# Sixteen batches through four conditioned blocks on one core: the second batch's weights kept in SBUF, and the last product of the third block as three products over rounded operands

## The chip, the cores and the metric

The program runs on one core of a Trainium2 chip. Time is the device time of one execution in microseconds (us); of several executions the median counts. The core's engines are called here as the profile calls them: PE is TensorE with its matmuls, PEld its weight loads, ACT is ScalarE, DVE is VectorE, POOL is GpSimd, and SP issues all DMAs of this kernel.

## What is computed

Sixteen batches (256 rows by 256 columns each) go through four blocks one after the other. A batch never meets another. Cut to what matters:

```python
# block A: weights of its own for each batch, made from cond (64 numbers a batch)
Wd_b = Wd + 0.1 * (cond @ Wdd.T + bdd)        # (16, 128, 256): 32768 numbers a batch
Wu_b = Wu + 0.1 * (cond @ Wdu.T + bdu)        # as many
x = x + relu(x @ Wd_b.T + bd) @ Wu_b.T + bu
x = (layernorm(x) * w + bias + tanh(cond @ lin_w.T + lin_b)) * w + bias
# third block: modulated attention with 16 heads of 16, then a feed-forward part
h = layernorm(x) * g1 + b1;  q, k, v = split(h @ W_qkv.T + b_qkv)
x = x + (softmax(q k' / 4) v @ W_o.T + b_o) * a1
h = layernorm(x) * g2 + b2
x = x + (gelu_tanh(h @ W_f1.T + b_f1) @ W_f2.T + b_f2) * a2      # 256 -> 1024 -> 256
# fourth block
u = (x * (scale * rsqrt(mean(x*x)))) @ up_w.T;  val, gate = split(u)   # 256 -> 2048
h = val * gelu(gate)
y = quantised(h) @ ternary(down_w).T + x
```

## The kernel before

**Operands.** Most products are wanted more exactly than one product of rounded operands gives. For these the operands are split: `hi` is the number rounded to the type F32R, `lo` what is left of it, and the function `three` (L500 to L505) adds three products, hi by hi, lo by hi and hi by lo. In the profile such a product shows as three matmuls "f32" of one instruction each at L504. A product of plain F32 operands is written as one matmul, and the profile counts two matmul instructions for each. The second feed-forward product of the third block (`c_g`, L713) is of that plain kind: 16 matmuls a batch, 32 instructions, 512 in all. The hi copy is made by ACT (`ACT.Copy` into an F32R tile), the lo part by POOL (`low_part`, a subtraction) for `hA`, `hC` and `hD`, the inputs of three products.

**Turns.** The work of a batch is cut in four stages: A (block A, the second block, and q, k, v), B (attention), C (output product, the feed-forward part) and D (fourth block). Turn t holds stage A of batch t, B of t-1, C of t-2 and D of t-3, so there are 19 turns, 0 to 18. In which order each engine does the slices of a turn is written by hand in the tables `HEAD` (turns 0 to 5), `FULL` (one table, for turns 6 to 12) and `TAIL` (12 to 18). A name such as `C.g0` is a slice: stage C, the quarter 0 of the last product. On PE the four slices `C.g0` to `C.g3` of `c_g` stand between slices of attention: `B.t` (scores, transposed), `B.o` (times v). `C.f0` to `C.f3` make the 1024 hidden columns, `C.ht` and `C.xt` are transposes, `D.u0` to `D.u3` the 2048 columns of block four, `D.qt` and `D.y` its last product, `A.down`, `A.up`, `A.ht`, `A.q`, `A.k`, `A.v` stage A. Engines wait for each other by semaphores that count the steps of a stage; the lists `ACT_C`, `POOL_C` and so on name the steps.

**ACT and DVE in a turn.** ACT takes the relu (`A.down`), the two norms (`lnb`), the modulations and hi copies (`ht`, `xt`), the tanh gelus (`C.f`, tile `G`), the exact gelus (`D.u`, tile `gl`), q and k (`A.q`, `A.k`), the exponentials (`B.t`) and the copies `D.qt`. DVE multiplies `gl` by the value half (`D.u`, step `h`, tile `hd`), quantises (`D.quant`), takes the maxima of the scores (`B.s`) and makes the lo parts of q and k. `D.qt0` on PE waits for step `h3` of DVE, which comes after `D.u3`. The gated output of `c_g` goes DVE (`gate2`) then POOL (`x3`).

**The head.** The weights of all batches are generated from `hyper` (16 chunks of 1 MB) into the tile `gen`, which lies where `wup_hi` will be. The first batch's share goes from `gen` to the tile `cur` in 16 small DMAs (`first_rows`). The whole of `gen` is then stored to DRAM in four DMAs of 1 MB (L402), and `cur` of every later batch is loaded from there (`load_weights`, L391) and combined with the shared part by DVE (`A.cur`, function `combine`, L1056). Then SP loads W_qkv, W_f1, W_up, W_f2 and W_down. Each of the first three has a hi copy on ACT (`W.qkv`, `W.fa`, `W.up`) and a lo part on DVE (L1040).

## Time and profile before

| what | us |
|---|---|
| median of 3 runs | 893.33 |
| lowest and highest of them | 892.43, 893.88 |
| the profiled execution | 892.32 |
| its span in the trace | 890.5 |
| PE busy in the span | 814.7 |
| PEld, DVE, ACT, POOL busy | 629.9, 551.0, 520.9, 235.1 |

The span is what the trace covers; 1.8 us of the profiled execution lie around it. PE's busy time is made of modelled ends, since matmuls are pipelined: how long a matmul really takes of PE is read from the distance of two starts, not from its duration. The granted clock of PE in forty slices is about 0.5 of full in the first tenth of the span, after its first two slices, and 1.0 from a fifth of it on.

### The profile page before, as it was taken

The page shows a single profiled execution, that of the slowest core. Times are in us where ns is not written, and L with a number is a line of the kernel's source. Part 1 is how long each engine was busy: PE and PEld are TensorE (multiplying, and loading weights), DVE is VectorE, ACT ScalarE, POOL GpSimd, SP SyncE. Part 2 cuts the span into 40 slices and gives each one's busy share as a digit, 9 for nine tenths or more (in the row PEclk, how much of TensorE's full clock was granted, in tenths as well). Part 3 has the DMA queues.
Part 4 walks back from the last instruction along what each step waited for, and adds up shares of the span by engine and source line. Part 5 has one row for each costly group of instructions (what it writes and reads, how often), then busy time and mean ns, then how long its engine had stood idle before and what let it go on. Part 6 is the DMA issues. An engine that isn't in the chain of part 4 may idle for free.

```text
span 890.5 us, 15833 instructions
## 1 busy us (share of the span) xinstructions
PE 814.7 (91%) x5852; PEld 629.9 (71%) x5852; DVE 551.0 (62%) x1063; ACT 520.9 (58%) x808; POOL 235.1 (26%) x333
## 2 busy tenths in 40 slices
PE   6862477999999999999999999999999999999976
PEld 4212346777787878787878787878788787877665
DVE  1322567686767768585858585858585767656424
ACT  1112243566676758585867667666667676765642
POOL 1002213050505142423223140505050505030310
PEclk9855577999999999999999999999999999999999
DMA  9989733334242342424251514234242333230100
GB/s 346 382 309 409 234 130 112 117 113 150 71 163 72 110 135 85 160 85 161 84 162 52 178 64 151 94 117 129 102 139 102 119 114 107 102 101 3 31 13 12
DMA packets 56093, 118.48 MB, mean 133 GB/s; under 512 B 6000, under 2 KB 11504, under 8 KB 53312
## 3 DMA queue, kind: packets, MB, share of 16 engines
q1 hardware_dynamic: 56016, 117.48, 38.7%
q8 instruction: 46, 0.75, 0.3%
q14 instruction: 31, 0.25, 0.1%
HBM read 82.51 MB, written 34.16 MB: 131 GB/s over the span
## 4 chain that ended last, share of the span: by engine, by line
PE 80%; issue 8%; DVE 4%; DMA 3%; POOL 3%; ACT 1%; SPq 1%; POOLq 0%; DVEq 0%; ACTq 0%
PE bank L504 31%; PE bank L713 13%; PE pair_s L668 6%; PE pair_t L504 5%; PE bank L679 3%; PE bank L760 3%; PE pair_s L656 3%; PE pair_s L634 3%; DMA hyp<-in_hyper 2%; PE bank L572 2%; PE bank L578 2%; PE pair_t L656 2%; PE bank L752 2%; PE pair_t L634 1%; PE pair_t L514 1%
## 5 line engine op out<-in xcount | busy, mean ns | idle before, releaser
L713 PE MATMUL bank<-wf,G 128*128 128x256 f32 x512 | 126.6, 391 | 0.7 <-ACT G L885 0.5
L504 PE MATMUL bank<-wup_hi,hD_hi 128*128 128x512 f32 x256 | 110.2, 430 | 4.1 <-POOL hD_lo L1333 3.2
L1361 POOL TENSOR_TENSOR x<-x,xcr 128x512 f32<-128x512 f32 x16 | 20.8, 1301 | 335.4 <-DVE x L1198 335.4
L870 ACT ACTIVATE Pr<-pair_s 128x1024 f32<-128x1024 f32 x64 | 65.6, 1025 | 74.8 <-PE pair_s L656 74.8
L713 PEld LDWEIGHTS bank<-wf,G 128*128 128x128 f32 x512 | 92.2, 189 | 21.8 <-issue 5.8
L504 PE MATMUL bank<-wup_hi,hD_lo 128*128 128x512 f32 x256 | 101.6, 397 | 0.0
L504 PE MATMUL bank<-wup_lo,hD_hi 128*128 128x512 f32 x256 | 101.5, 396 | 0.0
L1140 DVE TENSOR_REDUCE nmax<-pair_s 128x4 f32<-128x1024 f32 x64 | 77.9, 1218 | 20.4 <-PE pair_s L634 20.3
L1164 DVE STREAM_TRANSPOSE oq<-pair_s 128x512 f32<-128x512 f32 x32 | 22.9, 717 | 88.7 <-PE pair_s L668 88.7
L1140 DVE TENSOR_REDUCE nmax<-pair_t 128x4 f32<-128x1024 f32 x64 | 77.4, 1210 | 0.0
L914 ACT ACTIVATE gl<-bank,rsD 128x512 f32<-128x512 f32 x64 | 43.8, 684 | 52.7 <-PE bank L504 52.5
L1208 DVE SCALAR_TENSOR_TENSOR hd<-bank,rsD,gl 128x512 f32<-128x512 f32 x64 | 47.8, 747 | 32.0 <-PE bank L504 30.8
L668 PE MATMUL pair_s<-Pr,Va 128*32 128x256 f32 x1024 | 65.1, 396 | 0.3 <-ACT Pr L870 0.2
L870 ACT ACTIVATE Pr<-pair_t 128x1024 f32<-128x1024 f32 x64 | 65.2, 1019 | 0.0
L504 PEld LDWEIGHTS bank<-wup_hi,hD_hi 128*128 128x128 f32 x256 | 48.3, 189 | 18.8 <-POOL hD_lo L1333 3.4
L504 PEld LDWEIGHTS bank<-wup_lo,hD_hi 128*128 128x128 f32 x256 | 48.4, 189 | 11.7
L504 PEld LDWEIGHTS bank<-wup_hi,hD_lo 128*128 128x128 f32 x256 | 48.6, 190 | 9.7
L668 PEld LDWEIGHTS pair_s<-Pr,Va 128*32 128x32 f32 x1024 | 29.6, 112 | 26.6 <-ACT Pr L870 8.4
L922 ACT ACTIVATE qT<-bank 128x1024 bf16<-128x1024 bf16 x32 | 32.8, 1024 | 23.6 <-PE bank L752 23.6
L504 PE MATMUL bank<-hA_hi,wqkv_hi 128*128 128x256 f32 x128 | 39.9, 312 | 3.4 <-POOL hA_lo L1333 3.4
L504 PE MATMUL bank<-hC_hi,wf_hi 128*128 128x256 f32 x128 | 38.1, 298 | 3.6 <-POOL hC_lo L1333 3.6
L1333 POOL TENSOR_TENSOR hA_lo<-hA,hA_hi 128x512 fp32r<-128x512 f32 x16 | 20.6, 1285 | 75.9 <-ACT hA_hi L849 75.9
(183 smaller groups left out, 2000.4 us busy)
## 6 DMA issues: line engine op xcount, KB each, us to landing
hyp<-in_hyper SPq DMA_DIRECT2D x16, 1024.0 KB, 8.6
Qp<-qk_scratch SPq DMA_DIRECT2D x64, 256.0 KB, 4.9
Kp<-qk_scratch SPq DMA_DIRECT2D x64, 256.0 KB, 4.7
qk_scratch<-q_hi SPq DMA_DIRECT2D x16, 512.0 KB, 2.8
qk_scratch<-k_hi SPq DMA_DIRECT2D x16, 512.0 KB, 3.4
tC<-rows_scratch SPq DMA_DIRECT2D x16, 384.0 KB, 4.3
xT_t<-in_xT SPq DMA_DIRECT2D x16, 256.0 KB, 4.3
x_t<-in_x SPq DMA_DIRECT2D x16, 256.0 KB, 4.5
```

Of the source, the lines that this page charges most:

```text
L504: mm = pe.matmul(dst, l, r, start=first and i == 0, stop=last and i == 2)
L634: mm = pe.matmul(pair[p % 2][:, half, r * L:(r + 1) * L], Qp[lo:lo + KR, 1 - par, p, r * P:(r + 1) * P], Kp[lo:lo + KR, 1 - par, p, :], st ...
L656: mm = pe.matmul(pair[p % 2][:, half, k * L:(k + 1) * L], Kp[lo:lo + KR, 1 - par, p, k * P:(k + 1) * P], Qp[lo:lo + KR, 1 - par, p, :], st ...
L668: mm = pe.matmul(bank[1][32 * j:32 * j + 32, (g % 2) * L:(g % 2 + 1) * L], Va[:, 1 - par, k, 4 * g + j, :], Pr[:, (2 * g + j // 2) % 4, j ...
L679: mm = pe.matmul(bank[5][:, r * D:(r + 1) * D], oT[:, k, r * P:(r + 1) * P], wo[:, k, :], start=k == 0, stop=k == KT - 1)
L713: mm = pe.matmul(bank[5][:, r * D:(r + 1) * D], G[:, k, r * P:(r + 1) * P], wf2[:, k, :], start=k == 0, stop=k == FT - 1)
L760: mm = pe.matmul(bank[6][:, 0:D], qT[:, k, :], wq3[:, k, :], start=k == 0, stop=k == FT - 1)
L870: act.activation(Pr[:, p % 4, :, :].rearrange("p a n -> p (a n)"), pair[p % 2][:, :, :].rearrange("p a n -> p (a n)"), ACT.Exp, scale=DH * ...
L914: act.activation(gl[:, n % 2, :], bank[6][:, :], ACT.Gelu, scale=rsD[:, 1, n // 2:n // 2 + 1]).then_inc(act_d, 1)
L922: act.activation(qT[:, :, :].rearrange("p k n -> p (k n)"), bank[7][:, :].bitcast(BF16), ACT.Copy).then_inc(act_d, 1)
L1140: dve.tensor_reduce(nmax[:, n % 2, :, p % GP, :], pair[p % 2][:, :, :].rearrange("p a (r n) -> p a r n", r=RT), AX.X, ALU.max, negate=True ...
L1208: dve.scalar_tensor_tensor(hd[:, (n % 2) * HALF:(n % 2 + 1) * HALF], bank[7][:, :], rsD[:, 1, n // 2:n // 2 + 1], gl[:, n % 2, :], ALU.mul ...
```

## The change

There are four kinds of edits.

1. **The last feed-forward product in three.** `c_g` calls `three` with `G_hi`, `G_lo`, `wf2_hi`, `wf2_lo`. ACT copies `G` to `G_hi` in two halves (`C.gh0`, `C.gh1`), POOL subtracts in four quarters (`C.gl0` to `C.gl3`). W_f2 is split once, in turn 1 and 2 (`W.f2` on ACT and POOL). `C.g0` waits for the second quarter, `C.g1` for the fourth.
2. **The second batch's weights.** `first_rows` also copies the rows of batch 1 to a tile `second`, and `combine(1)` reads that. The DMAs of the first and of the second batch's rows stand side by side. The load of W_qkv is ahead of the last four of them. The stores of `gen`, W_f1 and W_up are issued within turn 0, W_f2 and W_down at the start of turn 1.
3. **Memory.** `hA`, `hC`, `hD`, `G` and the raw W_f2 lie on their lo parts, `sq` on `G_hi`, `gated` on `hC_hi`; `xcr` and `ys` are gone, and `x3` is used in their place. The ones beside v in `Va` are one column a head and no longer sixteen. POOL's `C.proj` therefore waits for the stores of the batch before last.
4. **Order.** The tables are new. In most turns PE does `C.f3` ahead of `B.m0` and `A.ht`, `D.qt0` ahead of `A.q`, and `B.t0` ahead of `A.v`.

```diff
-                        mm = pe.matmul(bank[5][:, r * D:(r + 1) * D], G[:, k, r * P:(r + 1) * P], wf2[:, k, :], start=k == 0, stop=k == FT - 1)
+                        mm = three(bank[5][:, r * D:(r + 1) * D], (G_hi[:, k, r * P:(r + 1) * P], G_lo[:, k, r * P:(r + 1) * P]),
+                                   (wf2_hi[:, k, :], wf2_lo[:, k, :]), k == 0, k == FT - 1)
...
+                    if n == 0:
+                        pe.wait_ge(pool_c, at(POOL_C, "glo1", c))
+                    elif n == 1:
+                        pe.wait_ge(pool_c, at(POOL_C, "glo3", c))
...
+                def c_gh(h):
+                    act.wait_ge(act_c, at(ACT_C, f"gelu{4 * h + 3}", c))
+                    act.activation(G_hi[:, 4 * h:4 * h + 4, :], G[:, 4 * h:4 * h + 4, :], ACT.Copy).then_inc(act_c, 1)
...
+                def c_gl(i):
+                    pool.wait_ge(act_c, at(ACT_C, f"ghi{i // 2}", c))
+                    pool.tensor_tensor(G_lo[:, 2 * i:2 * i + 2, :], G[:, 2 * i:2 * i + 2, :], G_hi[:, 2 * i:2 * i + 2, :].bitcast(F32),
+                                       ALU.subtract).then_inc(pool_c, 1)
+
+                def f2_weights():
+                    pool.wait_ge(act_w, at(ACT_W, "f2", 0))
+                    pool.tensor_tensor(wf2_lo[:, :, :], wf2[:, :, :], wf2_hi[:, :, :].bitcast(F32), ALU.subtract).then_inc(pool_w, 1)
...
                 sp.dma_start(cur[8 * c:8 * c + 8, :], gen[0:P:NB, c, :]).then_inc(first_in, 16)
+                sp.dma_start(second[8 * c:8 * c + 8, :], gen[1:P:NB, c, :]).then_inc(second_in, 16)
...
-                    dve.wait_ge(cur_in, 16 * b)
+                    dve.wait_ge(cur_in, 16 * (b - 1))
                 dve.wait_ge(dve_w, at(DVE_W, "base", 0))
-                dve.scalar_tensor_tensor(cur[:, :], cur[:, :], DELTA, base_c[:, :], ALU.mult, ALU.add).then_inc(cur_ready, 1)
+                dve.scalar_tensor_tensor(cur[:, :], second[:, :] if b == 1 else cur[:, :], DELTA, base_c[:, :], ALU.mult, ALU.add).then_inc(cur_ready, 1)
...
-                    past(pool, pool_c, POOL_C, "x3", c, 1)
-                    pool.tensor_tensor(xcr[:, :, :], xc[:, :, :], over_rows(tC[:, 2, :]), ALU.add).then_inc(pool_c, 1)
+                    if c >= 2:
+                        for r in range(RT):
+                            pool.wait_ge(y_out[r], 16 * (c - 1))
+                    pool.tensor_tensor(x3[:, par, :, :], xc[:, :, :], over_rows(tC[:, 2, :]), ALU.add).then_inc(pool_c, 1)
```

**DVE in the head**, from the end of batch 0's second norm on. `cur<-cur` is `combine(1)`, `q_lo` and `k_lo` are the lo parts that PE's `A.v` and the stores wait for, `wup_lo` is the lo part of W_up. Before:

```order
L1099 BN_AGGR mvA<-stA 128x2 x2
L1040 TENSOR_TENSOR wqkv_lo<-wqkv_raw,wqkv_hi 128x1536
L1056 SCALAR_TENSOR_TENSOR cur<-cur,base_c 128x512
L1132 SCALAR_TENSOR_TENSOR q_lo<-bank,small,q_hi 128x256 x2
L1040 TENSOR_TENSOR wf_lo<-wf_raw,wf_hi 128x2048
L1132 SCALAR_TENSOR_TENSOR k_lo<-bank,small,k_hi 128x256 x2
```

And now, up to the first maximum of turn 1:

```order
L1139 BN_AGGR mvA<-stA 128x2 x2
L1096 SCALAR_TENSOR_TENSOR cur<-second,base_c 128x512
L1077 TENSOR_TENSOR wqkv_lo<-wqkv_raw,wqkv_hi 128x1536
L1172 SCALAR_TENSOR_TENSOR q_lo<-bank,small,q_hi 128x256 x2
L1172 SCALAR_TENSOR_TENSOR k_lo<-bank,small,k_hi 128x256 x2
L1077 TENSOR_TENSOR wf_lo<-wf_raw,wf_hi 128x2048
L1146 TENSOR_TENSOR x<-bank,x_t 128x512
...
L1139 BN_AGGR mvA<-stA 128x2 x2
L1077 TENSOR_TENSOR wup_lo<-wup_raw,wup_hi 128x4096
L1180 TENSOR_REDUCE nmax<-pair_s 128x2x2
```

The combination for batch 1 reads `second`, W_f1's part is behind `k_lo`, and W_up's part (behind `q_lo` of turn 1 before) is ahead of the first maximum of turn 1.

**ACT in the middle of an inner turn**, from the first tanh gelus on. `x<-x,rsA` is the norm `A.lnb`, `gl` the gelu of `D.u3`. Before:

```order
L885 ACTIVATE G<-bank,small 128x256 x2
L832 ACTIVATE x<-x,rsA 128x256 x2
L885 ACTIVATE G<-pair_t,small 128x256 x4
...
L849 ACTIVATE hA_hi<-hA 128x512
L914 ACT_TABLE_LOAD
L914 ACTIVATE gl<-bank,rsD 128x512
L885 ACT_TABLE_LOAD
L885 ACTIVATE G<-bank,small 128x256 x2
L856 ACTIVATE q_hi<-bank,small 128x256 x2
L922 ACTIVATE qT<-bank 128x1024
L856 ACTIVATE k_hi<-bank,small 128x256 x2
```

And now:

```order
L917 ACTIVATE G<-bank,small 128x256 x2
L917 ACTIVATE G<-pair_t,small 128x256 x2
L865 ACTIVATE x<-x,rsA 128x256 x2
L922 ACTIVATE G_hi<-G 128x1024
L917 ACTIVATE G<-pair_t,small 128x256 x2
L860 ACTIVATE hA<-bank,mod 128x256 x2
L881 ACTIVATE hA_hi<-hA 128x512
L949 ACT_TABLE_LOAD
L949 ACTIVATE gl<-bank,rsD 128x512
...
L957 ACTIVATE qT<-bank 128x1024
L888 ACTIVATE q_hi<-bank,small 128x256 x2
L922 ACTIVATE G_hi<-G 128x1024
```

A copy of 128x1024 stands ahead of the gelus of `C.f2`, of A's modulation and of the gelu of `D.u3`; the second one is between q and k, and `D.qt0`'s copy has come ahead of q.

## Rows read from the trace of the kernel before

**Rows 1.** Stretches: length, busy of PE, PEld, DVE, ACT, POOL; clock, DMA share.
```profile
0.00:100.00 100.00, 57.53 (x238) 26.71 (x238) 23.99 (x51) 16.10 (x27) 12.35 (x23) 0.71 0.92 349
...
484.00:535.00 51.00, 51.00 (x391) 41.20 (x390) 35.90 (x68) 35.54 (x56) 14.34 (x20) 1.00 0.31 107
```
**Rows 2.** Costliest groups: busy us, mean ns of one, idle before.
```profile
L713 PE MATMUL bank<-wf,G 128*128 128x256 f32 x512 | 126.6, 391 | 0.7 <-ACT G L885 0.5 <-DVE k_lo L1132 0.3
...
L504 PEld LDWEIGHTS pair_t<-hC_hi,wf_lo 128*128 128x128 f32 x128 | 24.6, 193 | 0.0
```
**Rows 3.** PE in order of time, two inner turns: start, duration, line, tiles.
```profile
508.11 1.03 PE L572 MATMUL bank<-xT_t,cur 128*128 128x256 f32 x4
...
522.12 0.28 PE L504 MATMUL bank<-hC_hi,wf_hi 128*128 128x256 f32 x1
...
526.26 0.28 PE L504 MATMUL pair_t<-hC_lo,wf_hi 128*128 128x256 f32 x1
...
528.23 0.28 PE L504 MATMUL bank<-hC_lo,wf_hi 128*128 128x256 f32 x1
528.43 0.50 PE L634 MATMUL pair_s<-Kp,Qp 64*128 64x256 f32 x4
```
**Rows 4.** PE in order of time, round the first slice of the product.
```profile
539.43 1.99 PE L713 MATMUL bank<-wf,G 128*128 128x256 f32 x8
541.35 0.50 PE L656 MATMUL pair_s<-Qp,Kp 64*128 64x256 f32 x4
...
554.81 1.03 PE L572 MATMUL bank<-xT_t,cur 128*128 128x256 f32 x4
```
**Rows 5.** ACT in order of time, same turn: table, exact gelu, exponential.
```profile
529.02 1.28 ACT L914 ACT_TABLE_LOAD   x1
530.79 0.69 ACT L914 ACTIVATE gl<-bank,rsD 128x512 f32<-128x512 f32 x1 [0.50 <-PE bank L504]
...
539.31 1.03 ACT L870 ACTIVATE Pr<-pair_s 128x1024 f32<-128x1024 f32 x1 [0.80 <-PE pair_s L656]
```
**Rows 6.** DVE in order of time: step h3, and two twin steps of turn 2.
```profile
532.19 0.75 DVE L1208 SCALAR_TENSOR_TENSOR hd<-bank,rsD,gl 128x512 f32<-128x512 f32 x1 [0.85 <-PE bank L504]
...
146.79 0.87 DVE L1114 SCALAR_TENSOR_TENSOR x<-x,mvA,w_t 128x256 f32<-128x256 f32 x2
147.79 1.89 DVE L1121 SCALAR_TENSOR_TENSOR x<-x,rsA,tA 128x256 f32<-128x256 f32 x2
```
**Rows 7.** PE in turn 3, where `D.qt0` follows `B.s3` already.
```profile
205.11 0.40 PE L634 MATMUL pair_t<-Kp,Qp 64*128 64x256 f32 x4
205.69 0.62 PE L752 MATMUL bank<-identb,qi 128*128 128x128 bf16 x8 [0.18 <-DVE hd L1208]
```
**Rows 8.** POOL in order of time: inner turn, turn 2, and turn 0.
```profile
551.65 1.28 POOL L1361 TENSOR_TENSOR x<-x,xcr 128x512 f32<-128x512 f32 x1 [21.29 <-DVE x L1198]
...
148.12 1.28 POOL L1333 TENSOR_TENSOR hC_lo<-hC,hC_hi 128x512 fp32r<-128x512 f32 x1 [1.31 <-ACT hC_hi L879]
...
70.41 1.71 POOL L1301 TENSOR_TENSOR rsA<-mvA,eps_ln 128x2 f32<-128x2 f32 x1
```
**Rows 9.** PE in the head, turns 0 to 2.
```profile
93.76 0.58 PE L504 MATMUL bank<-wqkv_hi,hA_hi 128*128 128x256 f32 x1 [10.21 <-DVE q_lo L1132]
...
102.08 0.80 PE L634 MATMUL pair_s<-Kp,Qp 64*128 64x256 f32 x4
...
137.94 1.90 PE L679 MATMUL bank<-wo,oT 128*128 128x256 f32 x8
```
**Rows 10.** DVE in the head: the combination for batch 1, and W_up's lo part.
```profile
92.23 0.69 DVE L1056 SCALAR_TENSOR_TENSOR cur<-cur,base_c 128x512 f32<-128x512 f32 x1 [20.16 <-DMA cur<-cur_scratch]
...
121.72 4.40 DVE L1040 TENSOR_TENSOR wup_lo<-wup_raw,wup_hi 128x4096 fp32r<-128x4096 f32 x1
```
**Rows 11.** SP's issues: the load of batch 1's `cur`, and the store of `k_lo`.
```profile
77.56 0.34 SPq L391 DMA_DIRECT2D cur<-cur_scratch  x1
...
96.72 0.32 SPq L420 DMA_DIRECT2D qk_scratch<-k_lo  x1
```

235 lines of the change are left out of this document (131 added, 104 removed).

## Prediction, made before the run

> **What bounds the kernel now.** Read first the busy time of the engines by stretch [rows 1]: in the inner turns PE is busy in all 51.00 us of a 51 us stretch at full clock, DVE and ACT in 70% of it, POOL in 28%. That busy share is made of modelled ends, so the second thing to read is the distance of starts. A turn, from `A.down` to `A.down`, is 554.81 − 508.11 = 46.70 us [rows 3, 4], and in those rows one PE slice starts where the one before it ends. So in turns 3 to 15 what is taken from PE is taken from the time, unless a wait comes in its place. The head is another matter: in the first 100 us PE has work for 57.53 us at a mean clock of 0.71 while the DMAs are 92% busy [rows 1], and it stands still 10.21 us for `q_lo` [rows 9]. That wait is read through: `q_lo` is behind `combine(1)` on DVE, which itself waited 20.16 us for the load of `cur` [rows 10], and that load was issued at 77.56 [rows 11], behind 4 MB of stores, W_f1, W_up, W_f2 and W_down in SP's program.
>
> **The product in three (PE).** Before, a slice of four products holds PE from 539.43 to 541.35, 1.92 us or 0.24 for each of its 8 instructions [rows 4]; all 512 make 123 us. After, it is 12 matmuls of the shape that `C.f` has already, 128x256 with a new weight each. The 36 of `C.f0` to `C.f2` start 0.118 us apart (522.12 to 526.26 in 35 steps), but it is 0.20 where the attention's matmul follows (528.23 to 528.43), so the switch costs about 0.08 [rows 3]. A slice is 12 × 0.118 + 0.08 = 1.50 us: 0.42 less, and 1.7 us for the four slices of a turn. More instructions (768 for 512), less time.
>
> **What feeds it.** ACT gets two copies of 128x1024 a turn. None is in the trace; the exponential of that size takes 1.03 and a gelu of half the size 0.69 [rows 5]; I take 1.0 each. POOL gets four subtractions of 128x512 at 1.28 [rows 8], 5.1 us a turn; it was idle 21.29 us just ahead of `x3` [rows 8], where most of them go. `C.g1` waits for the fourth: from PE's end of `A.q` the chain is q's two copies 0.85, `gh1` 1.0, two subtractions 2.6 and some 0.4 of latencies, 4.9 us, while PE does `A.k`, `B.m1`, `D.y0`, `B.t0`, `A.v`, `C.g0` and `B.t1`, 6.7 us. Nothing waits. If `gh1` were 2 us later, `C.g1` would wait 0.2.
>
> **The new order in the turn.** The first copy, `gh0`, is ahead of the gelus of `C.f2`, of A's modulation and of `D.u3`'s gelu on ACT. Before, the table for that gelu began at 529.02 and the gelu waited for PE only 0.50 [rows 5]. With `C.f3` ahead of `A.ht` PE comes to `D.u3` at the same time as before, about 528.9, and is done with its first half at 530.3, but ACT, 1.0 us fuller and with the norm behind `C.f1`, loads the table at about 530.3 and gives the gelu from 531.6 to 532.3. `h3` on DVE takes 0.75 [rows 6] and ends at about 533.1. PE has done `D.u3` and `B.s3` by 532.4 and now wants `D.qt0` at once; before it had `A.q` there. So about 0.7 us of PE are lost. Turn 3 of before has this order: there 205.11 to 205.69 are 0.58 us where 0.33 are usual, a loss of 0.25, without the copy [rows 7]. Against that, `C.f2` with `C.f3` and `A.q` with `A.k` now stand together, which saves some switches: 0.3 us for four, and the remaining gaps of this stretch, 0.2. A turn gains 1.7 + 0.5 − 0.7 = 1.5 us. Bounds: 0.8, if the norm's delay of 1.2 (it stands behind `B.s3` on DVE) adds to the stall; 2.1, if the stall is the 0.25 of turn 3 or less. Other edits of the turn are at nothing: the aliasing puts waits on steps that ended a turn ago; POOL comes to its wait for the stores after `x2` of the next turn, when `D.y1` is past PE's `B.o1`, `C.xt`, `A.down`, `B.s0` and `C.proj`, and only the norm of C is queued behind it. Thirteen turns, 3 to 15: **19.5 us** (10.4 to 27.3).
>
> **Turn 2.** The same 1.7 for the product, and the norm of C is ahead of a maximum of 1.2 us on DVE; with `gh0` and the switch I take **2 us** (1 to 3.5). **Turns 16 and 17.** Turn 16 is PE-bound like the inner ones. In turn 17 the faster product starts later: `C.g1` must wait for two copies and two subtractions with little beside them (2 × 1.0 + 2.6 for 0.5 before). I take **1.6 us** for both (0 to 3).
>
> **The head.** With `second` in SBUF, DVE is free at 71 and `q_lo` follows `q_hi`, at about 83.4; `A.v` runs right behind `A.k` at 84.4 and not at 93.76. W_up ends in the queue by 81, as the four stores are served first and 2 MB of W_f2 and W_down are no longer ahead of q and k. `k_lo`, stored at 96.72 before, is ready at about 86.3, its loads land near 91.5, and `B.s0` of turn 1 can start at 92.6 for 102.08 [rows 9]: 9.5 us. Then some is given back. W_up's lo part, 4.40 us [rows 10], stood where DVE waited for `B.o0` and now stands ahead of the first maximum; `A.q` no longer stands ahead of `B.s3`, which gives 1.2. Left: 6.3 us at `C.proj` of turn 2 (137.94 before). POOL's part of W_f2 is 128x2048, four times a subtraction of 1.28, about 5 us, and falls on DVE's `B.o0`. Does it hold DVE? In turn 2 a DVE step whose twin takes 0.87 took 1.89 [rows 6] beside POOL's `hC_lo` [rows 8], and POOL's 128x2 step took 1.71 beside W_qkv's lo part [rows 8]. So it can hold the normalisation of `o0` and `k_lo` behind it, and `B.s0` of turn 2 may be 1 us late. I take **5.5 us** (2 to 9.4).
>
> The Trainium skill (SBUF — State Buffer, § Who interferes with whom) has a rule for this: VectorE and GpSimd share one pair of ports, the later instruction is blocked for the whole of the earlier one, and only VectorE instructions with two SBUF inputs, or in a 2-port mode, are concerned. Both held steps above are of that kind, so the trace agrees. By that rule the four new subtractions of a turn cost nothing, since maxima, `h` and the lo parts read PSUM; without it each could hold DVE for up to 1.0 us, 4 us a turn, of which DVE has 13 idle.
>
> **The sum.** 5.5 + 2 + 19.5 + 1.6 = 28.6 us. Against the profiled execution, 892.32 − 28.6 = 863.7; that execution is 1.0 below the median of the runs, so the median to expect is 893.33 − 28.6 = **864.7 us**.
>
> **Rivals.**
> *The stall of `D.qt0` doesn't come (chance 0.14).* The copy or the table is faster than I take it, and each turn gains 2.1: 13 × 0.6 more, with the better head 3 more: 854. For it: turn 3's loss was only 0.25. Against it: ACT's table load and the copy are in a row ahead of the gelu.
> *ACT becomes the bound (0.14).* `gh0` and `gh1` also push the exponentials: `B.t1` has to wait for the second of them, and the turn gains 0.8 or less. 893.3 − 4 − 1 − 10.4 − 1 = 877. For it: ACT has three tables a turn; against: it was idle in 30% of the stretch [rows 1], 14 us of a turn.
> *The head gives nothing (0.07).* The rows of batch 1 and W_qkv delay the first batch, or W_up's 4.40 us and POOL's 5 eat the rest: 893.3 − 23.1 = 870.
> *Slower: the weight loads set the pace (0.03).* A weight load of this shape is 193 ns long against a pace of 118 [rows 2, 3]. If it did not overlap with the matmul ahead of it, 768 would take 148 us for 123: 25 more, with nothing for the product (893.3 − 5.5 + 25) 913. It decides where the pace is over 0.118 + 28.6/768 = 0.155 us. Against it: `C.f` keeps its pace with the same loads.
> The Trainium skill (Perfetto Trace Analysis, § Identifying the Most-Contended Engine) measures PE's headroom by the busy share of the weight loads and not of the matmuls; by that the 256 added loads would count and the shorter matmuls would not, which is this rival. The rows of `C.f` speak against it here.
> *The edits cancel (0.02):* within 0.2%.
>
> **How the numbers follow.** Forecast 0.60, rivals 0.14, 0.14, 0.07, 0.03, 0.02. Within 0.2% of before (about 1.8 us) is what a measurement can't tell from no change. Faster 0.95, same 0.02, slower 0.03. The range takes in the forecast's bounds and the first three rivals without their ends: 852 to 877.
>
> **What would show it.** After: `A.down` to `A.down` of an inner turn 45.2 us; the new slice 1.50 us between starts and a pace of 0.118; a wait of PE for DVE's `hd` of about 0.7 ahead of `D.qt0`; no wait for `G_lo` outside turn 17; `A.v` of turn 0 at about 84, `C.proj` of turn 2 near 132.5; DVE's `on` of turn 1 longer than 0.42 beside POOL's part of W_f2. It is wrong if the pace of the new slice is above 0.13, if PE waits for POOL each turn, or if `C.proj` of turn 2 is later than 136.

## The result, and the profile after

| | median of its runs | lowest to highest | profiled execution (its span) |
|---|---|---|---|
| before | 892.88 us, 4 runs | 890.64 to 893.88 | 892.32 (890.5) |
| after | 879.67 us, 4 runs | 878.91 to 881.95 | 881.95 (880.1) |

The ratio is 0.9867, with a 95% interval of 0.9847 to 0.9887: 13 us faster, or 1.3%. The sign was right. The size was not: 28.6 us were forecast, and 879.67 lies above the range of 852 to 877. Six more runs of the changed kernel, on another chip (a0_after, below), gave 881.79 (879.38 to 882.47; ratio 0.9876), so the miss isn't one of measurement.

The busy time of the changed kernel by stretch: stretch, length, busy of PE, PEld, DVE, ACT and POOL, granted clock, DMA share, GB/s. They answer to [rows 1].

```profile
0.00:100.00 100.00, 56.42 (x250) 26.17 (x250) 30.67 (x65) 19.45 (x27) 15.62 (x27) 0.75 0.93 343
...
484.00:535.00 51.00, 50.77 (x419) 42.40 (x420) 37.25 (x76) 38.53 (x58) 21.94 (x26) 1.00 0.38 129
```

TensorE is still what bounds an inner turn, at full clock. ACT is 3 us busier in the 51 us, and POOL 7.6, but these windows begin at different places of a turn. Over one turn each (508.11 to 554.81 before, 501.31 to 547.04 after) it is 1.8 for ACT and 5.1 for POOL.

The product, in the costliest groups of the changed kernel (busy us, mean ns of one, idle before), where [rows 2] had 512 matmuls of 391 ns:

```profile
L528 PE MATMUL bank<-wf_hi,G_hi 128*128 128x256 f32 x256 | 76.9, 300 | 0.9 <-ACT G L917 0.8
L528 PE MATMUL bank<-wf_lo,G_hi 128*128 128x256 f32 x256 | 71.7, 280 | 0.0
L528 PE MATMUL bank<-wf_hi,G_lo 128*128 128x256 f32 x256 | 71.7, 280 | 0.0
```

These three groups show 768 matmuls, and of their little idle time most is for the gelus; the one wait for `G_lo` that the trace has is of 0.17 us, in turn 17. Their busy time is 220 us, more than the 126.6 of [rows 2], and yet the product is faster: each of these lasts 280 ns and the next starts 118 ns after it. The busy column says nothing here, the distance of starts everything.

PE of the changed kernel in order of time, one inner turn (start, duration, line, tiles): `A.down`, `A.ht`, `B.s2`, the second half of `B.s3`, `D.qt0`, `A.q`, `C.g0`, `B.t1`, `C.g1`, `B.o0`, and the next `A.down`. It answers to [rows 3, 4].

```profile
501.31 1.03 PE L596 MATMUL bank<-xT_t,cur 128*128 128x256 f32 x4
...
521.22 0.60 PE L609 MATMUL bank<-small,x 128*128 128x128 f32 x4
521.85 0.50 PE L658 MATMUL pair_s<-Kp,Qp 64*128 64x256 f32 x4
...
525.86 0.39 PE L658 MATMUL pair_t<-Kp,Qp 64*128 64x256 f32 x4
526.45 0.62 PE L781 MATMUL bank<-identb,qi 128*128 128x128 bf16 x8 [0.20 <-DVE hd L1248]
526.88 0.36 PE L528 MATMUL bank<-hA_hi,wqkv_hi 128*128 128x256 f32 x1
...
533.06 0.28 PE L528 MATMUL bank<-wf_hi,G_hi 128*128 128x256 f32 x1
...
534.55 0.50 PE L680 MATMUL pair_s<-Qp,Kp 64*128 64x256 f32 x4
...
535.22 0.39 PE L528 MATMUL bank<-wf_hi,G_hi 128*128 128x256 f32 x1
...
536.83 1.93 PE L692 MATMUL pair_s<-Pr,Va 128*32 128x256 f32 x32
...
547.04 1.03 PE L596 MATMUL bank<-xT_t,cur 128*128 128x256 f32 x4
```

A turn is 547.04 − 501.31 = 45.73 us for 46.70 before: 0.97 gained where 1.5 was forecast. `C.g0` takes 534.55 − 533.06 = 1.49 us, but `C.g1` 536.83 − 535.22 = 1.61, and `C.g2` and `C.g3` 1.60 each. The stall ahead of `D.qt0` is 526.45 − 525.86 = 0.59 us from the start of the second half of `B.s3` to that of `D.qt0`, where 0.33 are usual, so 0.26 and not 0.7. `A.ht` holds PE for 0.63 (521.22 to 521.85); in the kernel before it was 0.35, with `C.f3` behind it:

```profile
526.49 0.60 PE L585 MATMUL bank<-small,x 128*128 128x128 f32 x4
526.84 0.36 PE L504 MATMUL bank<-hC_hi,wf_hi 128*128 128x256 f32 x1
```

The two profiled executions, cut at the starts of `C.proj` of turns 2, 3 and 16 (before 137.94, 182.66 and 788.94; after 135.55, 182.49 and 778.03), give the four terms of the sum:

| term | forecast | measured |
|---|---|---|
| head, to `C.proj` of turn 2 | 5.5 (2 to 9.4) | 2.4 |
| turn 2 | 2 (1 to 3.5) | −2.2 |
| turns 3 to 15 | 19.5 (10.4 to 27.3) | 10.7 |
| turns 16, 17 and the end | 1.6 (0 to 3) | −0.5 |
| sum | 28.6 | 10.4 |

The sum of the right column is the difference of the two profiled executions (892.32 − 881.95). That of after is the slowest of its four, which is why it gives 10.4 where the medians give 13.2. A turn is counted here from `C.proj` to `C.proj`.

### The profile page after: what moved, and what is told of

Same layout as the page of the kernel before. It is cut to its first block, busy times and chain, and to the rows that moved or that the text cites. A ratio compares the mean times of both kernels' runs of the same rounds, so it can differ in the third digit from the quotient of the medians.

```text
span 880.1 us, 16405 instructions
## 1 busy us (share of the span) xinstructions
PE 798.5 (91%) x6108; PEld 634.1 (72%) x6108; DVE 555.9 (63%) x1063; ACT 554.7 (63%) x844; POOL 324.1 (37%) x398
## 4 chain that ended last, share of the span: by engine, by line
PE 77%; DVE 5%; issue 5%; ACT 4%; POOL 4%; DMA 4%; SPq 1%; POOLq 0%; DVEq 0%; ACTq 0%
PE bank L528 41%; PE pair_s L692 6%; PE pair_t L528 5%; PE bank L789 3%; PE pair_s L680 3%; PE bank L703 3%; DMA hyp<-in_hyper 2%; PE pair_s L658 2%; PE bank L781 2%; PE pair_t L680 2%; PE bank L596 2%; PE bank L602 1%; DVE nmax L1180 1%; PE pair_t L658 1%; DVE hd L1248 1%
## 5 line engine op out<-in xcount | busy, mean ns | idle before, releaser
L1398 POOL TENSOR_TENSOR G_lo<-G,G_hi 128x512 fp32r<-128x512 f32 x64 | 81.9, 1293 | 117.6 <-ACT G_hi L922 117.6
L1408 POOL TENSOR_TENSOR x<-x,gated 128x512 f32<-128x512 f32 x16 | 20.4, 1274 | 165.6 <-DVE gated L1238 165.6
L528 PE MATMUL bank<-wf_hi,G_hi 128*128 128x256 f32 x256 | 76.9, 300 | 0.9 <-ACT G L917 0.8
L949 ACT ACTIVATE gl<-bank,rsD 128x512 f32<-128x512 f32 x64 | 43.7, 683 | 45.2 <-PE bank L528 44.9
L528 PE MATMUL bank<-wf_lo,G_hi 128*128 128x256 f32 x256 | 71.7, 280 | 0.0
L528 PE MATMUL bank<-wf_hi,G_lo 128*128 128x256 f32 x256 | 71.7, 280 | 0.0
L528 PEld LDWEIGHTS bank<-wf_hi,G_hi 128*128 128x128 f32 x256 | 48.2, 188 | 8.1 <-issue 2.5
```

What stands on the lines that cost most here:

```text
L528: mm = pe.matmul(dst, l, r, start=first and i == 0, stop=last and i == 2)
L949: act.activation(gl[:, n % 2, :], bank[6][:, :], ACT.Gelu, scale=rsD[:, 1, n // 2:n // 2 + 1]).then_inc(act_d, 1)
L1398: pool.tensor_tensor(G_lo[:, 2 * i:2 * i + 2, :], G[:, 2 * i:2 * i + 2, :], G_hi[:, 2 * i:2 * i + 2, :].bitcast(F32), ALU.subtract).then_i ...
```

## Is it the product or the order: four corners

There are two theories of why a turn gained 0.97 and not 1.5. By the first, the product gives what its slices show, and the new order of the turn costs something. By the second, the product's feed (two copies on ACT, four subtractions on POOL) costs, in the stall at `D.qt0` above all. The first two runs take the product and the feed away, one at a time.

**e1_plain**, the product plain again under the new order:

```diff
-                        mm = three(bank[5][:, r * D:(r + 1) * D], (G_hi[:, k, r * P:(r + 1) * P], G_lo[:, k, r * P:(r + 1) * P]),
-                                   (wf2_hi[:, k, :], wf2_lo[:, k, :]), k == 0, k == FT - 1)
+                        mm = pe.matmul(bank[5][:, r * D:(r + 1) * D], G[:, k, r * P:(r + 1) * P], wf2[:, k, :], start=k == 0, stop=k == FT - 1)
```

with `C.gh0`, `C.gh1`, `C.gl0` to `C.gl3` and both `W.f2` out of the tables. What was expected:

> The changed kernel with its last feed-forward product back on plain fp32 operands: C.g reads G and wf2 as before the change, and the rounding of G (C.gh), its low halves (C.gl) and the two splits of W_f2 are gone; every other line and the order stay. Theory A (what the product is worth is what its slices show): the four slices of a turn go back from 1.49, 1.61, 1.60 and about 1.6 us to about 1.9 each, 1.27 us a turn, 20 us over 16 turns, less the 0.26 us stall ahead of D.qt0 that goes with C.gh0 (4 us): about 16 us slower than the changed kernel, 893 to 897 us, which puts the new order and the new head at about nothing beside the 893 of before. Rival B (the feed costs more on ACT and POOL than the one stall shows): the loss is under 10 us and the inner turn stays under 46.3. Rival C (the order was cut for the three-matmul product, so the plain one under it waits nowhere new): over 20 us, 900 or more.

Measured: 899.16 us (897.04 to 899.79, 4 runs), ratio 1.0085 (1.0057 to 1.0113): slower than before the change, and 19.5 us slower than after it. The inner turn is 47.01 us. So the product is worth 47.01 − 45.74 = 1.27 us a turn, as the slices say (7.59 us for the four before, 6.32 after). And with the same product as before, the new order is 0.31 us a turn slower than the old one (46.70). Theory A held in its mechanism. It subtracted 4 us for a stall that should go with the copy, and they were not there: the loss was 19.5 and not 16.

The slices of e1_plain also say what the forecast compared wrongly. PE of e1_plain, `C.g0` and the first matmul of `B.t1` behind it:

```profile
541.67 1.89 PE L739 MATMUL bank<-wf,G 128*128 128x256 f32 x8
543.49 0.51 PE L682 MATMUL pair_s<-Qp,Kp 64*128 64x256 f32 x4
```

Behind `A.v` a plain slice takes 543.49 − 541.67 = 1.82 us. `C.g1` and `C.g3`, behind slices of `B.t`, take 1.93 and 1.92 in the same turn, and `C.g2`, behind `D.qt1`, 1.88. So the plain product pays the same 0.11 for what stands ahead of it as the product in three does (1.49 and 1.61). Place by place the three matmuls save 0.32 or 0.33 us a slice, 0.28 in `C.g2`, and nowhere the 0.42 of the forecast.

**e2_nofeed**, the three matmuls with nothing that feeds them (both operands read the tile that the gelus write):

```diff
-                        mm = three(..., (G_hi[:, k, r * P:(r + 1) * P], G_lo[:, k, r * P:(r + 1) * P]),
+                        mm = three(..., (G_lo[:, k, r * P:(r + 1) * P], G_lo[:, k, r * P:(r + 1) * P]),
```

> The three matmuls of the product stay, and what feeds them goes: the gelus write the tile that TensorE reads for both operands, and C.gh0, C.gh1 and C.gl0 to C.gl3 are left out, so the low part of G is not made and the output is another. Order else unchanged. Theory A (the feed costs one stall a turn, ahead of D.qt0): the inner turn falls by 0.2 to 0.3 us from 45.74, 3 to 5 us in all, about 875.5. Rival B (ACT paces the front of the turn, so 2 x 0.9 us of rounding per turn are paid in more than one place: B.t, C.xt): the inner turn falls by 0.6 us or more, 870 or less. Rival C (the stall is the gelu table and the hd of VectorE, not C.gh0): no change, 879 to 880, and the wait for hd ahead of D.qt0 is still there.

Measured: 878.07 us (877.13 to 879.39, 4 runs), inner turn 45.76. Rival C: no change in the turn, and the wait ahead of `D.qt0` stands as it stood, with neither copy nor subtraction anywhere in the kernel. PE of e2_nofeed in order of time:

```profile
526.05 0.62 PE L779 MATMUL bank<-identb,qi 128*128 128x128 bf16 x8 [0.20 <-DVE hd L1246]
```

So the feed is free, all of it: 2.1 us of ACT (two copies of 1.06) and 5.1 of POOL in each turn cost PE nothing in an inner turn. The stall comes from the place of `D.qt0`. `D.qt0` waits for `h3`, whose row in the changed kernel is this:

```profile
525.65 0.75 DVE L1248 SCALAR_TENSOR_TENSOR hd<-bank,rsD,gl 128x512 f32<-128x512 f32 x1 [0.90 <-PE bank L528]
```

It begins 0.13 us behind the start of `B.s3` (525.52) and lasts 0.75, and PE has only `B.s3`, 0.67 us, to put beside it. Its wait is put down to PE's own matmuls of `D.u3`. ACT's gelu ends only 0.1 us ahead of it here, so this row alone doesn't decide between the two. But in e4_f3 (below) the gelu ends 0.6 us ahead of the step and the stall is the same 0.25. So it isn't ACT that sets it.

**e14_plain_old_front** is the fourth corner: the old front of the turn (see e6_lnb_f3 below) with the plain product.

> As e10_order_wup with the plain product in place of the three (as in e1_plain: no rounding of G, no low halves, no splits of W_f2). Theory A (product and order are independent, 1.27 us a turn for the one, 0.3 for the other): the inner turn is 46.70 to 46.80 and the time 20 us above e10_order_wup, 891 to 893. Rival B (part of what the old front gains is in the gaps around the new product): the inner turn is 47.0 as in e1_plain. Rival C (the rounding of G hinders somewhere in this order though it did not in the changed kernel's): under 46.5.

Measured: 890.93 us (889.57 to 899.25, 11 runs), inner turn 46.77. The periods of an inner turn, in us:

| | new front | old front |
|---|---|---|
| plain product | 47.01 (e1_plain) | 46.77 (e14_plain_old_front) |
| product in three | 45.74 (after) | 45.50 (e6_lnb_f3, e10_order_wup) |

The product is 1.27 in either column, the front 0.24 in either row. They are independent; theory A. The back of the turn, which e14_plain_old_front keeps new, makes up the remaining 0.07 to 46.70; no run takes it apart.

## What of the order costs

**e3_qt0**, `D.qt0` behind `A.q` again, on PE and ACT:

```diff
-... B.s3 D.qt0 A.q A.k ...
+... B.s3 A.q D.qt0 A.k ...
```

> The changed kernel with D.qt0 moved behind A.q on TensorE and on ACT in the eight turns' entries where it stands ahead of it (before the change it stood behind). Theory A (the stall ahead of D.qt0 is TensorE time that A.q can fill): the wait of 0.59 us from the last B.s3 matmul to D.qt0 shrinks to the 0.33 of before, the inner turn goes from 45.74 to about 45.5, 3 to 4 us in all, 876. Rival B (what D.qt0 releases, its copy on ACT and then D.y0, becomes late by the 1.2 us of A.q): no gain or a loss of up to 0.3 us a turn, 879 to 884, with a wait ahead of D.y0 or A.k instead.

Measured: 879.24 us (877.83 to 880.34, 4 runs), inner turn 45.60. The time can't be told from that of after; the period is 0.14 shorter in every inner turn. PE of e3_qt0, the first matmul of `A.q`, `D.qt0`, and the first of `A.k`:

```profile
523.55 0.38 PE L532 MATMUL bank<-hA_hi,wqkv_hi 128*128 128x256 f32 x1
...
525.08 0.62 PE L785 MATMUL bank<-identb,qi 128*128 128x128 bf16 x8
525.51 0.36 PE L532 MATMUL bank<-hA_hi,wqkv_hi 128*128 128x256 f32 x1
```

Theory A held for the wait, which is gone, 0.26 us. But `A.q` and `A.k`, which took 2.90 together, now take 1.53 and 1.51 around `D.qt0`: 0.14 goes back for the split. What is left is 0.12 to 0.14, and that is the measured gain.

**e4_f3**, `C.f3` on PE behind `B.m0` and `A.ht` again, nothing on ACT:

```diff
-... C.f2 C.f3 B.m0 A.ht B.s2 ...
+... C.f2 B.m0 A.ht C.f3 B.s2 ...
```

> The changed kernel with C.f3 moved back behind B.m0 and A.ht on TensorE in the seven entries where it stands ahead of them. Theory A (C.f3 is a filler: behind A.ht it covers the wait of B.s2 for the row maxima): in turn 2 the two waits of 0.86 and 0.54 us for nmax go, about 1 us or up to 2 with the low clock behind them; in the inner turns, where no such wait shows, nothing, 877.5 to 879.5. Rival B (ACT's C.f3 gelus start later by the 1 us, and C.gh1 and the exponentials B.t behind them): the inner turn is 0.2 to 0.6 us longer, 883 to 888. Rival C: each switch between the four row tiles and full matmuls costs, and this order has another one: 0.1 us a turn, 881.

Measured: 884.64 us (884.14 to 886.74, 5 runs), inner turn 46.21: 0.47 worse, the size of rival B but not its mechanism. PE of e4_f3, `B.m0`, `A.ht` and the first matmul of `C.f3`:

```profile
521.20 0.27 PE L668 MATMUL pair_s<-small,parts 128*32 128x128 f32 x1
521.83 0.66 PE L613 MATMUL bank<-small,x 128*128 128x128 f32 x4 [0.36 <-ACT x L869]
522.24 0.36 PE L532 MATMUL bank<-hC_hi,wf_hi 128*128 128x256 f32 x1
```

PE comes to `B.m0` and `A.ht` 1.4 us earlier than in the changed kernel and meets ACT, which has put the norm of A (`A.lnb`) behind the gelus of `C.f1`: `B.m0` and `A.ht` take 1.04 us, where it was 0.46 before the change and 0.73 in the changed kernel. That is 0.31 of the 0.47. The rest is `C.f3` split off again: 4.30 and 1.60 us for 5.75 together, 0.15, about what rival C said. Theory A failed in turn 2: its two waits for the row maxima are 0.86 and 0.54 us here too. The new order of ACT needs the new order of PE.

**e5_lnb** (e3_qt0 with ACT's `C.f1 A.lnb` as `A.lnb C.f1` again) and **e6_lnb_f3** (that and the edit of e4_f3):

> The changed kernel with D.qt0 behind A.q (as in the run e3_qt0, inner turn 45.60) and, on ACT, A.lnb ahead of C.f1's gelus again, as before the change (it stands behind them in the changed kernel). Theory A (A.ht on TensorE takes 0.63 us in place of 0.35 because it waits for the x that A.lnb writes, behind the two gelus of C.f1): A.ht goes back to 0.35 and the inner turn from 45.60 to 45.3, 4 us in all against e3_qt0: 875. Rival B (A.ht is longer because of what stands around it, fp32 four-row products behind and ahead, not by a wait): it stays 0.63, the inner turn 45.6, 879. Rival C (C.f1's gelus are late by A.lnb, and C.f3 on TensorE, which reuses a bank, waits): C.f grows by 0.3 us or more, 882.

> As e5_lnb, with C.f3 back behind B.m0 and A.ht on TensorE as well: the order of the front of the turn is then that of before the change on TensorE and on ACT, with C.gh0 between. Theory A (in e4_f3 it was A.lnb that made this order dear: B.m0 and A.ht together took 1.04 us there against 0.46 before the change): with A.lnb early they take 0.46 again and the inner turn is within 0.1 us of e5_lnb, 45.2 to 45.4. Rival B (the place of C.f3 itself costs, since its gelus and C.gh1 come a microsecond later): the inner turn is 0.3 us or more above e5_lnb.

Measured: e5_lnb 879.03 us (877.25 to 879.56, 4 runs), inner turn 45.60; `A.ht` stays 0.63. Rival B held, and my reading of `A.ht` was wrong: it doesn't wait for `x`. e6_lnb_f3: 877.20 us (874.97 to 879.27, 4 runs), inner turn 45.50, 0.1 below e5_lnb; `B.m0` and `A.ht` take 0.47 together, so theory A held in its mechanism and not in its 45.2 to 45.4. In e5_lnb `A.ht` starts at 519.13 and `B.s2` behind it at 519.76, as in the changed kernel (521.22 and 521.85). PE of e6_lnb_f3, `A.ht` and what follows it:

```profile
516.50 0.60 PE L613 MATMUL bank<-small,x 128*128 128x128 f32 x4
516.86 0.36 PE L532 MATMUL bank<-hC_hi,wf_hi 128*128 128x256 f32 x1
```

The same four matmuls, 0.60 us long in both kernels. A full 128x128 matmul of the product's kind starts 0.36 behind their start, the attention's 64-row one 0.63. So what stands behind a slice decides 0.27 us of it. From `C.f0` to the end of `B.s3` the changed kernel lost 0.44 us against before: 0.28 are this, 0.26 the stall at `D.qt0`, and 0.10 comes back because `C.f3` runs on from `C.f2` (5.75 for 4.26 and 1.59). Behind that, 0.17 more comes back, since `A.q` and `A.k` take 2.90 together for 1.50 and 1.57 around `D.qt0`.

**e12_adjacent** puts `C.g1` directly behind `C.g0`, to see whether 1.61 is the price of the neighbour:

```diff
-... C.g0 B.t1 C.g1 ...
+... C.g0 C.g1 B.t1 ...
```

> The changed kernel with C.g1 directly behind C.g0, and B.t1 behind both, in the eight entries that have C.g0 B.t1 C.g1. It is for the length of a slice, not for the time. Theory A (a slice is 12 matmuls at the pace of C.f, 1.50 us, and 1.61 where it follows products of four row tiles or transposes: the 0.11 is the price of the change between them): C.g1 takes 1.50 or less in its new place, and the inner turn falls by about 0.1 us if nothing waits, 878. Rival B (C.g1 takes 1.61 anywhere, for instance because POOL's C.gl2 and C.gl3 and the read of G share something): it stays 1.6. In either case B.t1 comes 1.5 us later; if its exponentials set the pace there, B.o0 waits up to that long and the inner turn grows to 46 to 47, up to 895.

Measured: 891.40 us (889.22 to 893.18, 12 runs), inner turn 46.63. The two slices (first start, and start of `B.t1` behind them), and where the time went:

```profile
538.50 0.28 PE L532 MATMUL bank<-wf_hi,G_hi 128*128 128x256 f32 x1
...
541.41 0.50 PE L684 MATMUL pair_s<-Qp,Kp 64*128 64x256 f32 x4
...
543.12 1.93 PE L696 MATMUL pair_s<-Pr,Va 128*32 128x256 f32 x32 [0.97 <-ACT Pr L906]
```

Two slices in 541.41 − 538.50 = 2.91 us, 1.46 each: theory A. In these rows a slice costs 1.50 or less only behind another full product of its kind, and 0.11 more behind the attention's tiles or a transpose, which is where three of the four stand. The arrangement can't be had, though: `B.t1` late by 1.5 us delays ACT's exponentials, `B.o0` waits 0.97 for them, and the whole gain of the change is gone. `B.t1` between the slices is no filler; it is what keeps ACT fed.

## The head

In the changed kernel the first batch starts later, and turn 1 is then faster. PE of the changed kernel: the last `generate`, `A.down` of turn 0, `A.v` of turn 0, `B.s1` of turn 1, `C.proj` of turn 2 (before: 54.89, 60.51, 93.76, 108.30 and 137.94; some of them in [rows 9]).

```profile
57.39 1.94 PE L538 MATMUL pair_t<-hyp,condbd 128*32 128x512 f32 x8 [1.05 <-DMA hyp<-in_hyper]
64.45 2.05 PE L596 MATMUL bank<-xT_t,cur 128*128 128x256 f32 x4 [5.13 <-DVE cur L1096]
...
87.81 0.34 PE L528 MATMUL bank<-wqkv_hi,hA_hi 128*128 128x256 f32 x1
...
103.78 0.80 PE L658 MATMUL pair_s<-Kp,Qp 64*128 64x256 f32 x4 [6.07 <-DVE nmax L1180]
...
135.55 1.89 PE L703 MATMUL bank<-wo,oT 128*128 128x256 f32 x8
```

From `A.down` of turn 0 to `C.proj` of turn 2 the change gains 77.4 − 71.1 = 6.3 us, the figure that the prediction worked out. But `A.down` of turn 0 starts 3.9 us late, and 2.4 are left. Two suspects for the rest: the 16 transfers of `second`, and W_up's low half, which stands ahead of the first maximum.

**e7_second**: the 16 transfers issued together behind the first batch's gates.

```diff
-                sp.dma_start(second[8 * c:8 * c + 8, :], gen[1:P:NB, c, :]).then_inc(second_in, 16)
 ...
             load_gates(0)
+            for c in range(NCH):
+                sp.dma_start(second[8 * c:8 * c + 8, :], gen[1:P:NB, c, :]).then_inc(second_in, 16)
```

> The changed kernel with the 16 transfers of the second batch's rows (second from gen) issued together behind the first batch's gates, not one with each chunk of the hypernetwork's weights. Theory A (in the stream they cost each chunk 0.35 us of DMA time, 3.00 us against 2.65 a chunk): the last generate ends near 54.9 rather than 57.4, A.down of turn 0 starts 3 us earlier, and all later turns with it, 876.5 to 877.5. Rival B (the chunks are slower because of W_qkv, x3 and the other early transfers, not because of these small ones): the pace stays 3.0 and nothing moves, 879 to 880. Rival C (the start comes back and turn 1 or 2 takes it again, since the next wait there, for the row maxima or the weights, is tied to something else): C.proj of turn 2 moves by less than half of what A.down of turn 0 does.

Measured: 885.02 us (883.69 to 885.96, 4 runs), 5.4 slower than after. PE, then ACT of e7_second:

```profile
60.10 2.04 PE L601 MATMUL bank<-xT_t,cur 128*128 128x256 f32 x4 [5.34 <-DVE cur L1101]
...
91.67 2.05 PE L601 MATMUL bank<-xT_t,cur 128*128 128x256 f32 x4 [6.35 <-ACT Va L898]
```

```profile
88.40 1.91 ACT L834 ACTIVATE wf_hi<-wf_raw 128x2048 fp32r<-128x2048 f32 x1 [5.96 <-DMA wf_raw<-in_w_f]
```

Its first half is theory A: without them in the stream a chunk takes 2.65 us for 3.02 (the last four starts of `generate`, 45.74 to 53.70 here, 48.33 to 57.39 in the changed kernel), and `A.down` of turn 0 is 4.35 us earlier. The rest is rival C: the transfers stand on SP's queue now, 10 us of issues. W_f1's load behind them is issued at 76.61, no earlier than the 75.77 of the changed kernel, though the batch that needs it is 4.35 us ahead. ACT waits 5.96 us for it ahead of `k_hi`, and turn 1 starts at 91.67 for 90.24.

**e8_wup**: W_up's low half on DVE behind `A.q` of turn 1, where it was before the change.

> The changed kernel with VectorE's low halves of W_up back behind A.q of turn 1, as before the change; in the changed kernel they stand ahead of B.s0 of turn 1 and take 4.65 us there. Theory A (the row maxima of turn 1, for which TensorE waits 6.07 us at B.s1, lie behind it): C.proj of turn 2 comes 3 to 4 us earlier, 876. Rival B (the maxima have another bound, the loads of K and Q that land at 96.9, and behind A.q the 4.65 us come ahead of B.o1, which the next turn waits for): under 1 us either way, 879 to 881.

Measured: 876.38 us (875.98 to 876.77, 4 runs), 3.3 better than after by the medians, 5.8 by the profiled executions. `B.s1` of turn 1 waits 1.48 us for the maximum, not 6.07, and `C.proj` of turn 2 starts at 129.93, 5.6 earlier. Theory A, and rather more of it than expected. The prediction had set the same edit down as a cost inside its 6.3; it never asked what the head would be without it. Its 6.3 came out by luck: without that cost its terms give 6.3 + 4.4 = 10.7 from `A.down` to `C.proj`, where e8_wup has 77.43 − 65.47 = 12.0, and the cost was 5.6 and not 4.4.

**e10_order_wup** joins e6_lnb_f3 and e8_wup; **e11_all** adds the late rows of e7_second with W_f1's load ahead of them; both ran on one chip with the changed kernel itself (**a0_after**).

> The changed kernel itself, unaltered, beside the others on one chip, so that differences under half a per cent are read against it and not across chips. Every theory expects 878.5 to 880.5, and an inner turn of 45.7 to 45.8.

> The front of the turn in the order of before (D.qt0 behind A.q, A.lnb ahead of C.f1, C.f3 behind A.ht, as in e6_lnb_f3) and VectorE's W_up behind A.q of turn 1 (as in e8_wup). Theory A (the two are apart in time and add): 2.5 us and 3.3 us, 873.5 to 874.5, with C.proj of turn 2 near 130 and an inner turn of 45.50. Rival B (what e8_wup gained at the start is handed back by turn 2 under the other order): C.proj of turn 3 is less than 4 us earlier than in e6_lnb_f3, 876.

> As e10_order_wup, with the second batch's rows issued behind the first batch's gates (as in e7_second), and W_f1's load ahead of them on SP's queue. Theory A (e7_second won 4.35 us at A.down of turn 0 and lost it again and more because W_f1's load stood behind 10 us of issues on that queue, and the rounding of W_f1 stands ahead of k_hi on ACT: 5.96 us of wait): the 4 us stay won, A.v of turn 0 near 83.5, K of turn 1 loaded near 93, 869.5 to 871. Rival B (SP's queue delays something else by then, the stores of q and k or W_up's load, so that turn 1 starts no earlier): as e10_order_wup, 873 to 875. Rival C (the 1 MB of W_f1 in the queue's front delays the second rows and with them combine(1) on VectorE, ahead of the low halves of W_qkv): A.q of turn 0 comes late, 876 or more.

Measured: a0_after 881.79 us (879.38 to 882.47, 6 runs), 1.3 above the range that was expected of it, with an inner turn of 45.76; e10_order_wup **872.41** (869.65 to 873.48, 5 runs), ratio to before 0.9777 (0.9755 to 0.9799); e11_all 875.48 (875.08 to 876.19, 4 runs). e10_order_wup is better than both kernels: 9.4 us under a0_after on the same chip, with an inner turn of 45.50 and `C.proj` of turn 2 at 129.76. Theory A: the two add. (Its profiled execution is the fastest of its five, 869.65, and has turn 2 at the full clock, of which below.) e11_all wins 4 us at the start once more (`A.down` of turn 0 at 60.51 for 64.86) and is 3.5 us late at `C.proj` of turn 2 (133.27): rival B's mechanism, at more than its price. PE waits 7.38 us for the first K; PE, then SP's issues of W_up, the store of `k_lo` and the first load of K and Q behind it.

```profile
99.92 0.79 PE L661 MATMUL pair_s<-Kp,Qp 64*128 64x256 f32 x4 [7.38 <-DMA Kp<-qk_scratch]
```

```profile
82.59 0.33 SPq L435 DMA_DIRECT2D wup_raw<-in_w_up  x1
...
86.35 0.79 SPq L445 DMA_DIRECT2D qk_scratch<-k_lo  x1
...
95.30 0.32 SPq L454 DMA_DIRECT2D Qp<-qk_scratch  x1
```

W_up's 2 MB are issued at 82.59, not 76.25, the stores of q and k behind them, and the first load is issued 8.9 us after the last of these stores, where it was 1.9 in the changed kernel. **e13_rows** orders the queue the other way: W_f1, the four stores, the 16 transfers, then W_up.

> As e10_order_wup; on SP's queue behind the first batch's gates now stand W_f1's load, the four stores of the generated rows, the 16 transfers of the second batch's rows and W_up's load, in this order, and VectorE combines the second batch's rows behind A.q of turn 0 rather than ahead of the split of W_qkv. Theory A (in e11_all the 4 us won at A.down of turn 0 were lost because W_up's load was issued at 82.6, so that the stores of q and k and ACT's rounding of W_up stood in its way): W_up is issued near 73, the first K of turn 1 is there by 93, C.proj of turn 2 near 126, 868 to 869. Rival B (turn 1 has a bound of its own, whatever the queue): C.proj of turn 2 at 129 to 130 as in e10_order_wup, 872.

Measured: 874.83 us (874.59 to 875.92, 4 runs). `C.proj` of turn 2 is at 132.89, so neither theory: the 16 transfers alone hold the queue for 12.8 us, W_up is issued at 80.24 all the same and the load of the next x at 83.13, and `A.down` of turn 1 waits 5.97 us for that.

```profile
66.07 12.79 SPq L426 DMA_DIRECT2D second<-gen  x16
80.24 0.35 SPq L429 DMA_DIRECT2D wup_raw<-in_w_up  x1
```

Three placings, three gains at the start against the kernel that each was made from (4.35 us in e7_second, 4.35 in e11_all, 3.6 in e13_rows), and at `C.proj` of turn 2 each is some 3 us behind that kernel. That the 16 transfers cost the stream is shown. That they could be had for nothing is not; with one queue and 16 transfers none of these places was free.

**e15_splits** moves the two weight splits of turn 1 apart: W_f2's on POOL to turn 2, W_up's on DVE behind `B.o1`. **e16_rows_splits** is that with e13_rows.

> As e10_order_wup, with GpSimd's low halves of W_f2 moved from the end of turn 1 to ahead of C.gl0 in turn 2, and VectorE's low halves of W_up from ahead of B.o1 of turn 1 to behind it. Theory A (in turn 1 they stretch what VectorE does for the attention: TensorE waits 1.84 us for oq at the second half of B.t, and on takes 4.55 us in place of 0.42): the wait falls to the 0.93 of the changed kernel, on to 0.42, and C.proj of turn 2 comes 0.9 us earlier or somewhat more, 871. Rival B (a transfer of that length costs wherever it stands: in turn 2 it is in the way of parts or of hA_lo, and TensorE waits at B.m0 or A.q): up to 3 us slower, 875. Rival C (all of it is hidden): 872.4.

> e13_rows and e15_splits together. Theory A (each is worth what it is alone): the gains add, 867 to 868. Rival B (the earlier turn 1 is bound by the splits of W_up and W_f1 on VectorE and ACT, which then lie in its way): no better than the better of the two.

Measured: 878.02 us (874.19 to 878.96, 5 runs) and 879.00 (878.63 to 879.49, 4 runs): rival B in the one, at 5.6 us for its 3, and what that lost swamps the rest in the other. In the changed kernel POOL's split held DVE in turn 1, DVE first and then POOL:

```profile
126.10 0.25 DVE L1206 RECIPROCAL rec<-oq 128x16 f32<-128x16 f32 x1
126.39 3.83 DVE L1212 TENSOR_TENSOR on<-oq,rec 128x256 f32<-128x256 f32 x1
```

```profile
125.40 4.53 POOL L1403 TENSOR_TENSOR wf_lo<-wf,wf_hi 128x2048 fp32r<-128x2048 f32 x1 [7.32 <-ACT wf_hi L847]
```

and in e15_splits it holds a step of 16 elements in turn 2, for which PE waits:

```profile
123.27 0.42 DVE L1216 TENSOR_TENSOR on<-oq,rec 128x256 f32<-128x256 f32 x1
...
148.64 3.82 DVE L1190 CAST parts<-nmax 128x16 fp32r<-128x16 f32 x1
```

```profile
153.73 0.28 PE L668 MATMUL pair_s<-small,parts 128*32 128x128 f32 x1 [2.89 <-DVE parts L1192]
```

With the split gone from turn 1, `on` is 0.42 us again, and PE's wait for `oq` falls from 1.84 to 0.93 as theory A said, but `C.proj` of turn 2 is at 132.45, 2.7 later. The clock hides the rest of the answer: of the 2.7, 1.0 is a later first batch, 1.0 `A.q` with `A.k` (5.29 us for 4.31 at a granted clock of 0.50 for 0.64), and 0.5 `B.o0` (4.26 for 3.77 at 0.66 for 1.00). e1_plain settles it, since it has no split of W_f2 anywhere: from the second half of `B.t` to `C.proj` of turn 2 PE takes 9.28 us there, and 9.34 in the changed kernel with `on` held. So in turn 1 the split was covered. In turn 2 it costs 2.9 us at `B.m0`, with 1.5 more at `A.q` and `A.k` at the lower clock (4.48 for 2.96). The place that the changed kernel gives it is the better one. The Trainium skill (SBUF — State Buffer, § Who interferes with whom) says that the later of a VectorE and a GpSimd instruction is shut out for the whole of the other, if VectorE's reads two operands from SBUF or runs in a 2-port mode. The trace agrees for `on` (two SBUF inputs), and for the `RECIPROCAL` with one, which runs in 0.25 us in the midst of POOL's 4.53. The cast `parts` has one input too and was held; whether it ran in a 2-port mode no trace here shows.

## Turn 2 and the end: the clock

Turn 2 lost 2.2 us. The runs split it. Its length, `C.proj` to `C.proj`, is 46.9 us in after, a0_after, e2_nofeed, e5_lnb, e7_second and e8_wup, and 45.0 in e3_qt0, e6_lnb_f3 and e10_order_wup, with 44.72 before. The stretch from the third maximum to `C.g0`, as windows of after, e3_qt0 and before:

```profile
157.00:165.00 8.00, 6.16 (x41) 5.51 (x41) 5.40 (x9) 3.82 (x8) 3.10 (x3) 0.79 0.56 164
```

```profile
158.00:166.00 8.00, 7.00 (x60) 6.26 (x61) 6.79 (x13) 5.28 (x10) 4.80 (x4) 1.00 0.73 231
```

```profile
159.00:167.00 8.00, 7.36 (x61) 6.39 (x59) 6.85 (x14) 5.26 (x9) 0.99 (x1) 1.00 0.12 42
```

The granted clock is 0.79 in the changed kernel, so part of the stretch runs at the lower of its two levels (1.2 GHz for 2.4), and 1.00 in the others. `A.q` and `A.k` take 4.12 us there and 2.95 in e3_qt0. What PE did just before is the same in both: two waits for the row maxima. These are the rows of the changed kernel, and the one of before, where `C.f3` stood between `B.s2` and `B.s3`:

```profile
157.84 0.51 PE L658 MATMUL pair_s<-Kp,Qp 64*128 64x256 f32 x4 [0.86 <-DVE nmax L1180]
158.88 0.80 PE L658 MATMUL pair_t<-Kp,Qp 64*128 64x256 f32 x4 [0.54 <-DVE nmax L1180]
```

```profile
159.85 0.50 PE L634 MATMUL pair_t<-Kp,Qp 64*128 64x256 f32 x4 [0.18 <-DVE nmax L1140]
```

The waits are 1.40 us after and 0.18 before. That `C.f3` covered them is a reading of these rows; e4_f3 and e6_lnb_f3 put it behind `A.ht`, ahead of `B.s2`, where it covers neither, and no run has it between the two. By the two groups of lengths, 1.9 of the 2.2 us belong to the clock, and with the clock up the turn is still no shorter than before, though its product gained 1.27. Why the level fell in some kernels and not in others of the same order is open: e10_order_wup and e11_all have one order in turn 2 and are 45.06 and 46.79 long. The three kernels at 45.0 have in common that the clock had been low sooner in the turn: it was 0.55 to 0.60 from 8 to 12 us behind `C.proj`, and 0.64 to 0.72 in the kernels with the slow `A.q` and `A.k`. But e4_f3, with 0.70 there, has both at full clock (2.92 us), so that isn't the whole of it. At the end it is the same in little: the last `D.y` takes 1.89 us after and 1.05 before.

```profile
875.50 1.89 PE L789 MATMUL bank<-wq,qT 128*128 128x256 bf16 x8 [1.12 <-ACT qT L957]
```

## Why the prediction was wrong

- **The product, 1.7 us a turn: mis-sized.** The mechanism was right and the pace of 0.118 too. The step that failed is "12 × 0.118 + 0.08 = 1.50" for all four slices, set against 1.92 for each. It counts the change behind a slice and leaves out the one ahead of it, 0.11 us, which the old 1.92 holds. 1.50 is right for `C.g0` (1.49), whose neighbour ahead is `A.v`. The others are 1.60 to 1.61, and one of the old slices was 1.83. The trace of before showed it: there `C.f3`, 12 such matmuls behind `A.ht`, holds PE from 526.84 to 528.43 [rows 3], 1.59 us. Measured: 1.27 a turn, under the new front and under the old one. Over 16 turns this is 7 us, the largest part of the miss.
- **"0.5" for the order: wrong in sign.** It was a count of switches saved. e1_plain shows that the whole new order, its stall included, costs 0.31 where the prediction had −0.7 + 0.5 = −0.2. The two errors nearly cancel: the stall was 0.26 and not 0.7, and the four switches gave back 0.27, near the 0.3 counted for them, but 0.28 went at `A.ht`, whose follower I hadn't looked at, and the 0.2 for "the remaining gaps" had nothing behind it.
- **The cause of the stall: wrong.** I laid it on `gh0` and the table load on ACT. e2_nofeed has no `gh0` and the same stall; e3_qt0 has `gh0` and none. In e4_f3 the gelu is ready 0.6 us early, and the stall stays: what `D.qt0` waits for is DVE's 0.75 us behind PE's own `D.u3`, with only `B.s3` beside it. Turn 3 of before, with 0.25 in [rows 7], had it right, and I argued it away as "without the copy". The rival without the stall (854) fell with it: the stall was as small as it wanted, and the turn still gained 0.96.
- **Turns 4, 5 and 15**, taken as inner ones, gained 1.15, 0.62 and −0.58 us. That is 1.7 less than three inner turns at 0.96. They have orders of their own, which I didn't price and no run takes apart.
- **Turn 2, 2 us: wrong in sign, −2.2.** The product gained 1.27 there. The step that failed is taking over "the same 1.7" as if PE bound this turn as it does the inner ones: the new order leaves 1.4 us of waits for the maxima where 0.18 were, and behind them the clock was at its lower level (in a0_after too), which cost 1.9.
- **The head, 5.5 us: inside its bounds, for the wrong reason.** What was worked out, 6.3 from `A.down` to `C.proj`, came out at 6.3. The two sizes under it were both off and nearly cancel (see e8_wup), which is luck. The 0.8 taken off for POOL's part of W_f2 was not there: `on` was held, and PE didn't feel it. The 3.9 us of a late first batch were not in the sum but only in a rival of 0.07.
- **The end, 1.6 us: −0.5.** Turn 16 gained 1.2. From `C.proj` of turn 17 to the end it lost 1.7, of which 0.84 is the last `D.y` at the lower clock, 0.4 the `D.qt1` ahead of it (2.15 us for 1.74), and 0.55 lies between `C.proj` and `D.y1` of turn 17 (29.77 us for 29.22); `D.u` of turn 18 gives 0.1 back. In that stretch of turn 17 the product gives nothing: it is 29.79 with the plain product (e14_plain_old_front) and 29.72 with the three (e10_order_wup), because the slices, 0.7 us shorter together, start later behind waits for the gelus, `qT` and `G_lo`.
- **The range, 852 to 877: too narrow for its own terms.** It is said to take in the forecast's bounds, but the four lower ones add up to 2 + 1 + 10.4 + 0 = 13.4 us, which is 879.9. The measured 879.67 is there.
- **Right:** that ACT and POOL would carry the feed unseen in the inner turns, that the weight loads don't set the pace, that PE never waits for `G_lo` outside turn 17, that `on` would be held (3.83 us for 0.42), and the sign.

## What to carry to other kernels

When a bound engine's instruction is replaced by a cheaper form, price each place where it stands by its two neighbours, and set the new form against the old one in the same place: here 0.11 us for the neighbour ahead, in three slices, and 0.27 for the one behind `A.ht` make 0.6 us a turn, where 0.97 were gained. A change that brings a new form of a product and a new order should be split on the chip first, since the product was worth 19.5 us here, and with everything else of the change but without it the kernel was 7 us slower than before. And a start that is made faster by clearing the stream is not won until everything that was moved has a place on the queue: count the issues (0.6 us each for the small transfers in e7_second, 0.8 in e13_rows), and follow what is queued behind them.

## What was not expected of the hardware

- Sixteen small transfers from SBUF to SBUF slowed a stream of 1 MB loads from 2.65 to 3.02 us a chunk; issued in one go they took 12.8 us of the queue.
- The same four matmuls of `A.ht` free PE after 0.36 or 0.63 us, by what follows: a full matmul of rounded operands (e6_lnb_f3), or one on 64 rows (e5_lnb).
- A slice of the last product takes 0.11 us more behind the attention's matmuls than behind a full product of rounded operands, in either form (1.93 and 1.82 plain, 1.61 and 1.49 in three).
- TensorE's granted clock in turn 2 differed between kernels with the same instructions just before (0.79 and 1.00 over 8 us), for 1.9 us of 45.
